# An 8 MB adapter weight loaded in 32 chained transfers instead of four, in a kernel of an LSTM and an adapter

## The reference, cut to what matters

```python
xz = jnp.einsum('ntd,dk->ntk', x, Wx) + b
def step(carry, xz_t):
    prev_h, prev_c = carry
    z = xz_t + prev_h @ Wh
    ai, af, ao, ag = jnp.split(z, 4, axis=1)
    next_c = sigmoid(af) * prev_c + sigmoid(ai) * tanh(ag)
    next_h = sigmoid(ao) * tanh(next_c)
...
x = x + hs
```

```python
c = layernorm(cond) * gamma + beta
h = gelu(c @ W1 + bias1)
w = h @ W2 + bias2                      # W2: 256 x 8192, 8 MB
a1, b1, a2, b2 = [t.reshape(B, D, R) for t in jnp.split(w, 4, axis=-1)]
u = einsum('btd,bdr->btr', x, a2)
mid = gelu(x @ base_down + einsum('btr,blr->btl', u, b2))
v = einsum('blr,btl->btr', b1, mid)
out = x + mid @ base_up.T + einsum('bkr,btr->btk', a1, v)
```

## Time and profile before

| | us |
|---|---|
| median of 3 runs | 605.48 |
| lowest and highest run | 603.7, 606.89 |
| the profiled execution, its own time | 607.91 |
| its span, first to last instruction | 605.7 |

### The profile page before, as it was taken

How to read it: one execution, slowest core, us unless ns; L and a number is a source line. 1 busy time by engine, 2 the same in 40 slices (tenths; PEclk the granted TensorE clock), 3 DMA queues, 4 the chain that set the end, 5 groups by cost and what they waited for, 6 DMA issues and landing times.

```text
span 605.7 us, 34198 instructions
## 1 busy us (share of the span) xinstructions
PE 586.7 (97%) x14092; PEld 437.7 (72%) x14092; DVE 501.5 (83%) x2805; ACT 384.6 (63%) x2154; POOL 49.7 (8%) x96
## 2 busy tenths in 40 slices
PE   8698999999999999999999999999999999999997
PEld 5564567777777777777777777777777777777885
DVE  2577888888888888888888888888888888888873
ACT  1365566666666666666666666666666666666673
POOL 5001320000000000000000000000000000000000
PEclk9799999999999999999999999999999999999999
DMA  7889340232323113233311232322133233113201
GB/s 193 218 219 311 68 56 15 36 55 56 56 56 52 32 31 56 55 56 56 56 32 28 56 55 56 55 47 39 29 57 55 55 56 53 34 30 45 56 21 29
DMA packets 32142, 39.74 MB, mean 66 GB/s; under 512 B 3906, under 2 KB 29810, under 8 KB 30963
## 3 DMA queue, kind: packets, MB, share of 16 engines
q1 hardware_dynamic: 31282, 36.51, 30.3%
q0 software_dynamic: 704, 1.05, 1.2%
HBM read 16.05 MB, written 4.19 MB: 33 GB/s over the span
## 4 chain that ended last, share of the span: by engine, by line
PE 95%; issue 1%; DMA 1%; DVE 1%; POOL 1%; SPq 0%; ACT 0%; POOLq 0%; ACTq 0%
PE z L677 36%; PE x_bank L481 19%; PE z_o L677 9%; PE aux L507 8%; PE out_bank L531 7%; PE aux L492 3%; PE aux L459 3%; PE out_bank L563 2%; PE aux L514 2%; PE out_bank L606 1%; DMA seed<-proj 1%; PE out_bank L552 1%; PE x_bank L552 1%; DMA x_nat<-in_x 0%; PE x_bank L507 0%
## 5 line engine op out<-in xcount | busy, mean ns | idle before, releaser
L677 PE MATMUL z<-wh,h_t 128*16 128x96 f32 x8160 | 235.3, 249 | 3.5 <-issue 3.1
L677 PEld LDWEIGHTS z<-wh,h_t 128*16 128x16 f32 x8160 | 153.2, 96 | 109.5 <-DVE h_t L855 79.6
L830 DVE STREAM_TRANSPOSE z<-z 128x96 f32<-128x96 f32 x512 | 152.8, 299 | 73.3 <-PE z L677 47.6
L404 ACT ACTIVATE gates<-z 128x48 f32<-128x48 f32 x512 | 108.1, 211 | 122.6 <-DVE z L830 122.3
L481 PE MATMUL x_bank<-wx,x_t 128*128 128x256 f32 x512 | 156.3, 393 | 0.5 <-ACT x_t L336 0.5
L342 ACT ACTIVATE z<-seed 128x96 f32<-128x96 f32 x512 | 127.0, 248 | 5.8 <-DMA seed<-proj 5.8
L677 PE MATMUL z_o<-wh,h_t 128*16 128x64 f32 x4080 | 104.9, 219 | 0.1
L840 DVE SCALAR_TENSOR_TENSOR prod<-gates 128x32 f32<-128x32 f32 x512 | 98.7, 193 | 0.0
L481 PEld LDWEIGHTS x_bank<-wx,x_t 128*128 128x128 f32 x512 | 81.3, 197 | 5.9 <-issue 1.5
L677 PEld LDWEIGHTS z_o<-wh,h_t 128*16 128x16 f32 x4080 | 80.0, 97 | 0.6 <-issue 0.5
L346 ACT ACTIVATE z_o<-seed 128x64 f32<-128x64 f32 x256 | 58.4, 228 | 19.3
(11 more groups left out here) (125 smaller groups left out, 518.9 us busy)
## 6 DMA issues: line engine op xcount, KB each, us to landing
seed<-proj SPq DMA_DIRECT2D x128, 128.0 KB, 4.4
w<-in_L_cond_W SPq DMA_DIRECT2D x4, 2048.0 KB, 10.6
x_nat<-in_x SPq DMA_DIRECT2D x32, 128.0 KB, 4.3
out<-y_nat SPq DMA_DIRECT2D x32, 128.0 KB, 4.2
wx<-in_L_cond_Wx SPq DMA_DIRECT2D x2, 512.0 KB, 4.9
wh<-in_L_cond_Wh SPq DMA_DIRECT2D x2, 256.0 KB, 6.6
wh<-in_L_cond_Wh SPq DMA_DIRECT2D x1, 512.0 KB, 5.8
w_bias<-in_L_cond_bias POOLq DMA_DIRECT2D x4, 128.0 KB, 6.8
```

The source lines that it names most:

```text
L404: act.activation(gates[s % 2][m][:, 0:3 * B].rearrange("p (g b) -> p g b", b=B), zt[m].rearrange("p (g c) -> p g c", c=C)[:, :, 0:B], ACT. ...
L677: ins = pe.matmul(dst, h_prev[:, kc, :], rhs, start=False, stop=(kc == 1), skip_group_check=True)
L830: dve.transpose(zt[m], z_bank[m][:, 0:GC]).then_inc(turned[m], 1)
```

## The change

W2 comes in 16 pieces, one for each of TensorE's 16 weight steps, and a piece in two halves of 64 partitions, 256 KB each with rows of 1 KB. SP issues a half only when the same half of the piece before has landed. All pieces stand behind the seeds of block 1: P0 and P1 ahead of `load_x(3)`, P2 to P6 between it and `load_seed(2)` in block 0, P7 to P12 ahead of `load_seed(3)` in block 1, P13 to P15 ahead of `load_seed(4)` in block 2. TensorE waits for both halves of each piece. `W_FIRST` is 9, so the weight matmuls stand in steps 9 to 24; DVE's additions, the transpositions and the ACT copies follow. POOL places one quarter in block 0, two in block 1 and one in block 2. The waits for `b2_t` and `a1_t` move to the first matmul that reads them and are made once.

```diff
--- before.py
+++ after.py
@@ -39,7 +39,7 @@
 XW = G * H // XQ
 LN_EPS = 1e-5
 QUARTERS = (2, 1, 3, 0)
-W_FIRST = 7
+W_FIRST = 9
 W_COLS = D * RANK // NQ
 W_HALF = W_COLS // 2
 
@@ -143,7 +143,7 @@
         zeroed = sem("zeroed")
         w_loaded = {n: sem(f"{n}_loaded") for n in
                     ("wx_if", "wx_og", "wh", "b", "down", "up", "ln", "cond", "w1")}
-        w2_loaded = [sem(f"w2_loaded{q}") for q in range(4)]
+        w2_loaded = [[[sem(f"w2_loaded{q}_{i}_{r}") for r in range(2)] for i in range(NQ)] for q in range(4)]
         w_bias_zeroed, w_bias_loaded = sem("w_bias_zeroed"), sem("w_bias_loaded")
         w_placed = [sem(f"w_placed{q}") for q in range(4)]
         wx_ready, wh_ready = sem("wx_ready"), sem("wh_ready")
@@ -270,10 +270,19 @@
                 sp.dma_start(dst[:, :, lo:lo + n], src.rearrange(by_half, m=NM)[:, :, src_lo:src_lo + n])\
                   .then_inc(w_loaded[name], 16)
 
-            w2_q = W2.rearrange("(k p) (q n) -> q p k n", p=P, q=4)
-
-            def load_w2(q):
-                sp.dma_start(w2[q][:, :, :], w2_q[q]).then_inc(w2_loaded[q], 16)
+            w2_parts = W2.rearrange("(k p) (q j h n) -> q h k p j n", p=P, q=4, j=NQ, n=W_HALF)
+
+            def load_w2(piece):
+
+                n, i = divmod(piece, NQ)
+                q, (h, kc) = QUARTERS[n], divmod(i, 2)
+                if piece == 3 * NQ:
+                    sp.wait_ge(w_psum, 2)
+                for r, rows in enumerate((slice(0, P // 2), slice(P // 2, P))):
+                    if piece > 0:
+                        sp.wait_ge(w2_loaded[QUARTERS[(piece - 1) // NQ]][(piece - 1) % NQ][r], 16)
+                    sp.dma_start(w2[q][rows, kc, :].rearrange("p (j h n) -> p h j n", j=NQ, n=W_HALF)[:, h],
+                                 w2_parts[q, h, kc, rows]).then_inc(w2_loaded[q][i][r], 16)
 
             load_x(Blk(0, 0))
             sp.dma_start(b_row[:, :], b.rearrange("(a n) -> a n", a=1)).then_inc(w_loaded["b"], 16)
@@ -292,22 +301,19 @@
             sp.dma_start(b1_col[:, :], bias1.rearrange("(k p) -> p k", p=P),
                          allow_slow_non_contiguous=True).then_inc(w_loaded["w1"], 16)
             load_cols(up_raw, base_up, 0, 0, D, "up")
-            load_w2(QUARTERS[0])
             load_seed(Blk(0, 1))
             load_cols(down, base_down, 0, 0, D, "down")
 
             def one_block(k, front):
+                if not k.at_least(1):
+                    load_w2(0)
+                    load_w2(1)
                 if k.plus(3).exists():
                     load_x(k.plus(3))
-                if not k.at_least(1):
-                    load_w2(QUARTERS[1])
-                if k.k == 1:
-                    sp.wait_ge(w_psum, 2)
-                    load_w2(QUARTERS[3])
+                for piece in {0: range(2, 7), 1: range(7, 13), 2: range(13, 4 * NQ)}.get(k.k, ()):
+                    load_w2(piece)
                 if front:
                     load_seed(k.plus(2))
-                if not k.at_least(1):
-                    load_w2(QUARTERS[2])
                 done = follower(k.plus(-1))
                 if done and done.seq.exists():
                     store_y(done)
@@ -371,7 +377,7 @@
                 if k == 0 and s in (4, 5):
                     act.wait_ge(up_psum, s - 3)
                     act.activation(up_t[:, s - 4, :], out_bank[:, 0:D], ACT.Copy).then_inc(up_ready, 1)
-                if k == 2 and s in (0, 4):
+                if k == 2 and s in (1, 5):
                     n = s // 4
                     act.wait_ge(wt_psum, n + 1)
                     act.activation((a2_w, b1_w)[n][:, :, :], aux[:, 0:2 * P].rearrange("p (l t) -> p l t", l=2),
@@ -431,7 +437,7 @@
 
                     if s == 0 and not k.at_least(1):
                         evacuate_x(k.plus(2))
-                    if not k.at_least(EARLY + 1):
+                    if not k.at_least(EARLY + 2):
                         make_weights(k.k, s)
                     if s == 2 and e:
                         gelu_mid(e)
@@ -498,9 +504,10 @@
                 for i in parts:
                     l, part = divmod(i, 3)
                     if i == 0:
-                        pe.wait_ge(w_placed[3], W_PLACED)
                         pe.wait_ge(w_loaded["down"], 16)
                         pe.wait_ge(u_ready[a.lane], a.seq.k + 1)
+                    if i == 2 and a.blk.k == EARLY:
+                        pe.wait_ge(w_placed[3], W_PLACED)
                     cols = slice(l * P, (l + 1) * P)
                     lhs, rhs = ((down[:, part, cols], a.xp[:, part, :]) if part < 2 else
                                 (b2_t[:, cols], u_own[a.lane][:, :]))
@@ -523,8 +530,11 @@
                         if a.seq.at_least(1):
                             pe.wait_ge(y_copied[a.lane], a.seq.k)
                         pe.wait_ge(up_ready, 2)
+                        if a.blk.k == EARLY:
+                            pe.wait_ge(w_biased, 4 * NQ // 2)
+                        pe.wait_ge(v_ready[a.lane], a.seq.k + 1)
+                    if i == 2 and a.blk.k == EARLY:
                         pe.wait_ge(w_placed[0], W_PLACED)
-                        pe.wait_ge(v_ready[a.lane], a.seq.k + 1)
                     cols = slice(m * P, (m + 1) * P)
                     lhs, rhs = ((up_t[:, part, cols], act_t[a.lane][:, part, :]) if part < 2 else
                                 (a1_t[:, cols], v_own[a.lane][:, :]))
@@ -599,15 +609,15 @@
                         pe.wait_ge(up_ready, 2)
                     elif kc == 0:
                         pe.wait_ge(w_biased, 2 * n + h)
-                    if i == 0:
-                        pe.wait_ge(w2_loaded[q], 16)
+                    for half in w2_loaded[q][i]:
+                        pe.wait_ge(half, 16)
                     for j in range(NQ):
                         first = W_COLS * j + W_HALF * h
                         ins = pe.matmul(out_bank[32 * j:32 * j + B, 0:W_HALF], hid[:, kc, :],
                                         w2[q][:, kc, first:first + W_HALF], start=(kc == 0), stop=(kc == 1))
                     if kc == 1:
                         ins.then_inc(w_psum, 1)
-                if k == 2 and s in (0, 4):
+                if k == 2 and s in (1, 5):
                     n = s // 4
                     pe.wait_ge(w_placed[QUARTERS[n]], W_PLACED)
                     if n == 0:
@@ -869,8 +879,8 @@
                     dve.wait_ge(cond_t_psum, 1)
                     dve.tensor_copy(c_t[:, :, :], aux[:, 0:2 * B].rearrange("p (k b) -> p k b", k=2))\
                        .then_inc(cond_t_ready, 1)
-                if k > 0 and s % 2 == 0:
-                    u = ((k - 1) * TB + s) // 2
+                u, between = divmod(k * TB + s - W_FIRST - 1, 2)
+                if 0 <= u < 2 * NQ and not between:
                     n, h = divmod(u, 2)
                     dve.wait_ge(w_psum, u + 1)
                     if u == 0:
@@ -978,9 +988,8 @@
 
             def one_block(k, front):
                 add_h(k)
-                if k.k in (0, 1):
-                    place_w(2 * k.k)
-                    place_w(2 * k.k + 1)
+                for n in {0: (0,), 1: (1, 2), 2: (3,)}.get(k.k, ()):
+                    place_w(n)
 
             schedule(one_block)
```

## The result

| | us |
|---|---|
| before, median of 4 runs (603.7 to 607.58) | 606.18 |
| changed, median of 4 runs (629.49 to 630.59) | 629.79 |
| ratio, with its 95% interval | 1.0396 [1.0359, 1.0433] |
| span of the profiled execution, before and after | 605.7, 627.6 |

The change makes the kernel 4% slower, 23.6 us, where 4.3 us were forecast with a range up to 616. At the start of step 25 the changed kernel is 22.4 us behind (108.94 against 86.52): all of the loss lies ahead of it (the spans of the two profiled executions differ by 21.9 us).

What follows compares the result with a forecast made beforehand. The serial recurrence was taken as the bound, so effects were read at the start of step 25: 9.6 us of chain lateness minus 5.3 of stalls removed, +4.3, gave a median of 609.8 us, range 601 to 616.

Steps and rivals of the forecast that it cites:

- L: Full latency of one piece in SP's chain, from issue to landing and next issue: 2.3 to 3.1 us, taken as 2.9.
- The 0.43 for the second 128 KB: Most that the second 128 KB of a 256 KB half adds to its latency, at 300 GB/s: 0.43 us.
- the bound of 3.4: Latency of a piece where an instruction packet, holding one DMA engine about 1.1 us, delays the slowest part: 3.4 us.
- 14 us per us: Price at step 25 of each us of piece latency, as most of 16 links and three loads are in line.
- x of block 3: Its load, issued behind P1's halves, lands at 42.1 us, 0.9 late for step 7; net cost 0.6 us.
- x of block 4: Its load, behind P6 and the seeds of block 2, comes 2.3 us late for TensorE in step 15.
- P13 behind the seeds of block 3: P13 lands at 84.5 us, behind those seeds and x; step 22 wants it at 80.2: 4.3 us late.
- The three stalls go: TensorE's instruction-fetch stalls in steps 7, 12 and 14 vanish with the 2 MB transfers: 4.26 us gained.
- 1.02 more goes: TensorE's wait for `xp` in step 24 vanishes, as `place_w(3)` moves behind block 2's additions on POOL: 1.02 us gained.
- The first and second: Pieces keep up, latency 2.37 or less, 601.5 us, chance 0.30; it evens out, latency 2.37 to 2.8, 605.5, chance 0.24.
- The third: TensorE's idle wait in step 22 lowers its clock, up to 3.4 us more, 613 to 617 us; chance 0.08.
- The fourth: Instruction-fetch stalls stay, as the chain has 512 KB under way: up to 4.3 us more; no chance of its own.

Runs made afterwards that it cites:

- the quiet load of 128 KB: Kernel before with loads of W2 added in quiet stretches, six steps into a block; 128 KB over 64 partitions took 0.7 us more than the 2.2 of 64 KB.
- the quiet pair: Kernel before with two halves of 256 KB of W2 added in a quiet stretch, issued 0.7 us apart: 3.8 us for the pair.
- POOL's order: Kernel before with POOL's order alone changed, placements of the last quarter behind the additions of block 2: 606.17 us beside 607.66, ratio 0.9965.
- the filled version: Changed kernel with extra matmuls, never read, ahead of TensorE's five longest waits in steps 7, 15, 19, 21 and 22: 631.76 us, ratio 1.0394.

## Why the prediction was wrong

**The step that failed is the size of L**, "So L lies between 2.3 (second half hidden) and 3.1 us, and 3.4 ...", "I take 2.5 ... + 0.43 = 2.9". A lone half takes 3.6, and in the chain a link took 4.3 on average (worked out below), above even the upper bound. Three things went into it wrongly. The 0.43 for the second 128 KB came from a rate of transfers over 128 partitions; over 64 it is 0.7. The base, 2.3 and 2.70 for 128 KB, was too low as well: the quiet load of 128 KB took 2.9. And in the chain a link took another 0.7 us above the lone half, which the 2.9 had at nothing and only the bound of 3.4, for an instruction packet, allowed for; the quiet pair took 3.8, so 0.2 of it comes with the second half, and the cause of the rest stays open.

**The path was right, link by link.** The forecast gave landings, and the chain that ended last has them: P0 at 39.06 (38.9 forecast), P7 at 70.59 (63.1), P13 at 99.53 (84.5), P15 at 108.37 (90.3); P12 was there for TensorE at 92.86 (77.6). The link with the seeds of block 3 in line, P12 to P13, took 6.7 us where 6.9 were forecast. So nearly all of the 18 us by which P15 missed lie in the 13 links that have no seeds in line: 1.4 us each, which makes L 4.3. By the prediction's 14 us per us that is 4.3 + 14 x 1.4 = 23.9 us (its own lines have 13 such links, so 22.5); 22.4 were measured at step 25. The places of the waits were the ones named: x of block 3 (0.9 us late forecast, 3.09 of idle measured), x of block 4 (2.3, 5.29), P13 behind the seeds of block 3 (4.3, 4.17). The waits for the pieces ahead of it in steps 19 to 21 were larger (1.6, 6.4), as by P12 five links without seeds had gone by since P7.

**The gain was real.** "The three stalls go" and "1.02 more goes" nearly held: one gap by issue of 0.74 us stayed, above the 0.5 allowed for, and no wait for `xp`. Leaving three of the 2 MB transfers out (6 us, 4.9 of it in steps 7 to 24) and POOL's order (1 to 3 us) measured the two parts; 4.26 and 1.02 had been forecast. In the changed kernel the gain only lengthened the waits, since the chain sets the start of step 25.

**The rivals.** The first and second fell with L. The third was half right: the clock did fall after the wait in step 22, and after three others, but it cost nothing that the filled version could win back. The fourth, that the stalls stay, did not happen under the chain, and did in part as soon as more was under way (3.0 to 9.7 us by "issue").

**The rule against the split.** Whole pieces were 4 us (one under way) and 5.7 us (1 MB under way) better than halves. By that, the traces agree with the Trainium skill, page "DMA: Bandwidth & Descriptors", section "Rules for kernel authors", which says not to split a transfer into partition halves. The fit in its section on the anatomy of one DMA, given for the other kind of queue, would have made L 2.6 us for 256 KB, an estimate; the quiet half took 3.6, so here the measurement decides.

## What to carry to other kernels

A transfer that waits for the one before costs its whole round trip, issue to landing, and here 2.2 us of 3.6 were there with a quarter of the bytes; count links in line times that time against what the consumer asks for, and measure the round trip with the real shape in a quiet stretch. Keep as many bytes under way as the pace needs and no more (here 1 MB), whole over all partitions, and start early where the DMA engines stand idle. When a forecast of a chain misses, compare it landing by landing; the rows of the issuing queue stop at the last issue. A wait that moves from x to W2 when the order changes marks the chain as the bound, not the queue.

## What the runs showed of the hardware

- A load with rows of 1 KB took the same 3.6 us for 256 KB over 64 partitions and for 512 KB over 128; over 64 partitions 64 and 128 KB took 2.2 and 2.9 (one load of each, in a quiet stretch).
- 32 transfers of 256 KB with rows of 1 KB, issued without waits, came with more idle time of TensorE by issue than four of 2 MB: 9.7 us against 3.8. In 15 us with the DMA engines busy all the time the kernel's queue moved 2.72 MB with them and 4.58 with the 2 MB transfers.
- A loss of clock can be free: with five waits filled with matmuls, the mean granted clock of a kernel that waits for transfers rose from 0.978 to 0.992, and the time stayed.
